# GpSimd masks the bias in seven of sixteen heads, conditions load packed, and the first values are projected behind the keys

## What is computed

```
emb = silu(sin_emb(timestep)) @ W_ada + b_ada         # timestep: one number a sample
scale, shift = split(emb)
h = ln(x) * (1 + scale) + shift
q, k, v = h @ Wq + bq, h @ Wk + bk, h @ Wv + bv       # 16 heads of 16
s = q k^T / sqrt(16) + attention_bias[b, head]        # 512 x 512 for each sample and head
s = where(mask[b], -inf, s)                           # one mask for all heads of a sample
x1 = h + softmax(s) v @ Wo + bo
```

## Time and profile before

| | us |
|---|---|
| three runs, median (lowest to highest) | 1149.35 (1147.81 to 1149.48) |
| the profiled execution | 1147.64 |
| its span, first to last instruction | 1145.8 |
| busy: PE, DVE, ACT, GpSimd | 1026.5, 818.1, 776.6, 349.4 |

### The profile page before, as it was taken

How to read it: one execution, slowest core, us unless ns; L and a number is a source line. 1 busy time by engine, 2 the same in 40 slices (tenths; PEclk the granted TensorE clock), 3 DMA queues, 4 the chain that set the end, 5 groups by cost and what they waited for, 6 DMA issues and landing times. The chain is left out here.

```text
span 1145.8 us, 21120 instructions
## 1 busy us (share of the span) xinstructions
PE 1026.5 (90%) x6128; PEld 670.0 (58%) x6128; DVE 818.1 (71%) x2056; ACT 776.6 (68%) x1238; POOL 349.4 (30%) x464
## 2 busy tenths in 40 slices
PE   2599999999999999999999999983999989898862
PEld 2456556656656565655655665642777767676641
DVE  5586775876787777778678686764456978897665
ACT  2287877887787788778788787863457565765442
POOL 0205114213312322320511511004455555654421
PEclk9799999999999999999999999996999999999976
DMA  7787976986995995896796797641111110101001
GB/s 237 241 299 262 353 274 232 367 294 225 338 326 191 340 349 204 305 356 233 275 362 245 250 371 266 247 151 37 38 37 38 37 55 18 55 18 37 19 19 37
DMA packets 131288, 230.23 MB, mean 201 GB/s; under 512 B 8992, under 2 KB 58016, under 8 KB 127136
## 3 DMA queue, kind: packets, MB, share of 16 engines
q1 hardware_dynamic: 131232, 229.59, 56.8%
HBM read 187.62 MB, written 41.94 MB: 200 GB/s over the span
## 5 line engine op out<-in xcount | busy, mean ns | idle before, releaser
L679 DVE CUSTOM_DVE_ANT_0 prob<-s_bank,big 128x512 f32<-128x512 f32 x512 | 344.8, 686 | 128.7 <-PE s_bank L540 103.0
L820 ACT ACTIVATE prob<-prob,nmax 128x512 f32<-128x512 f32 x512 | 359.6, 722 | 36.4 <-DVE nmax L679 35.2
L549 PEld LDWEIGHTS t_bank<-ident,prob 128*128 128x128 f32 x2048 | 241.0, 141 | 196.7 <-issue 71.2
L549 PE MATMUL t_bank<-ident,prob 128*128 128x128 f32 x2048 | 316.0, 277 | 8.0 <-DVE pt L688 4.7
L827 ACT COPY pt<-t_bank 128x512 f32<-128x512 f32 x320 | 185.1, 578 | 98.6 <-PE t_bank L549 98.0
L539 PE MATMUL s_bank<-stack_k,stack_q 128*128 128x512 bf16 x512 | 195.6, 382 | 4.6 <-DVE nmax L679 2.6
L540 PE MATMUL s_bank<-mterm_early,ident_bf 128*128 128x512 bf16 x448 | 170.8, 381 | 0.0
L688 DVE COPY pt<-t_bank 128x512 f32<-128x512 f32 x192 | 132.0, 687 | 48.9 <-PE t_bank L549 48.9
L562 PE MATMUL o_bank<-pt,val 128*32 128x512 f32 x1024 | 135.8, 604 | 0.7 <-ACT pt L827 0.7
L1624 POOL TENSOR_TENSOR gl<-big,gh 128x512 fp32r<-128x512 f32 x64 | 87.1, 1372 | 86.3 <-DVE gh L1329 86.3
L939 POOL TENSOR_SCALAR val<-vst 128x64 f32<-128x64 f32 x128 | 27.0, 245 | 251.8 <-PE o_bank L562 217.9
(11 more groups left out here) (176 smaller groups left out, 1620.1 us busy)
## 6 DMA issues: line engine op xcount, KB each, us to landing
big<-in_fside_Bx16xSxS SPq DMA_DIRECT2D x128, 1024.0 KB, 6.6
pieces_dram<-pieces SPq DMA_DIRECT2D x64, 384.0 KB, 7.8
stack_q<-pieces_dram SPq DMA_DIRECT2D x16, 1024.0 KB, 8.0
stack_k<-pieces_dram SPq DMA_DIRECT2D x16, 1024.0 KB, 8.7
pieces_dram<-pieces SPq DMA_DIRECT2D x32, 256.0 KB, 7.5
xin<-in_x SPq DMA_DIRECT2D x8, 512.0 KB, 6.6
x_dram<-x SPq DMA_DIRECT2D x8, 512.0 KB, 2.6
big<-x_dram SPq DMA_DIRECT2D x8, 512.0 KB, 3.5
```

Source lines behind the costliest of these rows:

```text
L549: last = pe.transpose(t_bank[n % 2][:, c * P:(c + 1) * P], prob[:, n % NT, c * P:(c + 1) * P], ident[:])
L679: dve.tensor_tensor_reduce(out=prob[:, n % NT, :], in0=s_bank[n % 3][:, :], in1=bias[:, h % NB, t, :], scale=-1.0, scalar=3e38, op0=ALU.ad ...
L820: act.activation(tile, tile, ACT.Exp, bias=nmax[:, n % NT:n % NT + 1], scale=-1.0).then_inc(exped.sem, 1)
```

## The change

Three things are changed; lines are those of the kernel before.

1. **Masking.** The heads 1, 2, 3, 12, 13, 14 and 15 get no mask product on TensorE. For them GpSimd adds the mask term to the head's bias in its buffer, one operation of 128x2048 (`mask_bias`), placed at iterations -3, 1, 6, 42, 46, 50 and 54 of GpSimd's order, and DVE waits for it in place of the bias's landing. There is one mask term left, made after step 56's value copies; it serves all of the sample.
2. **Conditions.** The host packs the token numbers into one array, and angles, frequencies, pairs and four bias vectors into another. Two DMAs in place of eight, and the three for bq, bk and bo go too. W_ada is loaded behind x and waited for by PE alone.
3. **First values.** Before the loop, DVE takes the values' banks between its cuts (V0 behind K0's, V1 behind Q1's), and the low part of Wv is made before them. PE's order is the same, but it no longer waits for DVE's last cut there.

```diff
+POOL_MASKED = [1, 2, 3, 12, 13, 14, 15]
+MASK_AT = [-3, 1, 6, 42, 46, 50, 54]
+PE_MASKED = [h for h in range(H) if h not in POOL_MASKED]
+TERM_AT = 56
...
     def load(sp):
-        for dst, src in conds:
-            sp.dma_start(dst, src).then_inc(cond_in, 16)
+        sp.dma_start(toks[:], d["toks"]).then_inc(vecs_in, 16)
+        sp.dma_start(vecs[:], d["vecs"]).then_inc(vecs_in, 16)
+
+    def load_weights(sp):
+        sp.dma_start(w_ada, v["W_ada"]).then_inc(w_ada_in, 16)
...
-        dve.wait_ge(cond_in, 16 * len(conds))
+        dve.wait_ge(vecs_in, 32)
...
             def load_mask(b):
-                sp.wait_ge(late_term.sem, late_term.at(b, QT))
+                sp.wait_ge(term_done.sem, term_done.at(b - 1, QT))
...
             def scores(b, n):
-                if n < QT:
-                    pe.wait_ge(early_term.sem, early_term.at(b - 1, n + 1))
-                if h == EARLY_HEADS:
-                    pe.wait_ge(late_term.sem, late_term.at(b, t + 1))
+                by_pe = h in PE_MASKED
+                if h == PE_MASKED[0]:
+                    pe.wait_ge(term_done.sem, term_done.at(b - 1, t + 1))
...
-                pe.matmul(bank, stack_q[:, h, t * P:(t + 1) * P], stack_k[:, h, :], start=True, stop=False)
-                pe.matmul(bank, ident_bf[:], mterm[:, t, :], start=False, stop=True).then_inc(scored.sem, 1)
+                last = pe.matmul(bank, stack_q[:, h, t * P:(t + 1) * P], stack_k[:, h, :], start=True, stop=not by_pe)
+                if by_pe:
+                    last = pe.matmul(bank, ident_bf[:], mterm[:, t, :], start=False, stop=True)
+                last.then_inc(scored.sem, 1)
...
             def add_bias(b, n):
-                if t == 0:
+                if t == 0 and h in POOL_MASKED:
+                    dve.wait_ge(masked.sem, masked.at(b, POOL_MASKED.index(h) + 1))
+                elif t == 0:
                     dve.wait_ge(bias_in[h % NB], b * (16 * H // NB) + 16 * (h // NB + 1))
...
-            for m, use in enumerate(banks.uses):
-                if use in VALUES:
-                    dve.wait_ge(weights_in, 16 * len(later))
...
+            spare_use(banks, at["XT", 0], -1, first=True)
+            spare_use(banks, at["XT", 1], -1, first=True)
+            low_parts(-1)
+            dve.wait_ge(weights_in, 16 * len(later))
+            dve.wait_ge(w_high, 3)
+            dve.tensor_tensor(wl["wv"][:], w["wv"], wh["wv"][:], ALU.subtract).then_inc(w_low, 1)
+            cut(0)
+            cut(1)
+            spare_use(banks, at["V", 0], -1, first=True)
+            cut(2)
+            spare_use(banks, at["V", 1], -1, first=True)
+            cut(3)
...
+            def mask_bias(b, h):
+                pool.wait_ge(bias_in[h % NB], b * (16 * H // NB) + 16 * (h // NB + 1))
+                if h == POOL_MASKED[0]:
+                    pool.wait_ge(term_done.sem, term_done.at(b - 1, QT))
+                apart(pool, pool_apart)
+                pool.tensor_tensor(bias[:, h % NB], bias[:, h % NB], mterm[:], ALU.add).then_inc(masked.sem, 1)
```

More of the change, by code:

```diff
@@ L90, in load_layouts @@
         v[w] = d["L0_cond_" + w].rearrange("(c p) n -> p c n", p=P)
-    for w in BY_FEATURE:
+    for w in BY_FEATURE[len(VECTORS):]:
         v[w] = d["L0_cond_" + w]
@@ L193, in sines_of @@
         act.wait_ge(sines, 1)
-        act.activation(k["trig"][:], arg[:], ACT.Sin).then_inc(sines, 1)
+        act.activation(k["trig"][:], arg, ACT.Sin).then_inc(sines, 1)
         act.wait_ge(sines, 2)
@@ L205, in modulate @@
         last.then_inc(ada_done, 1)
-    return dict(load=load, angles=angles, domains=domains, rotations=rotations, modulation=modulation,
+    return dict(load=load, load_weights=load_weights, angles=angles, domains=domains, rotations=rotations, modulation=modulation,
                 sines_of=sines_of, modulate=modulate)
@@ L942, in copy_values, with mask_term @@
                 last.then_inc(val_done.sem, 1)
-            def early_mask_term(b, t, first=False):
+            def mask_term(b, t, first=False):
                 if t == 0:
@@ L978, in iteration @@
                         copy_values(b, VALUES_AT.index(n))
-                    if n == LATE_TERM_AT:
+                    if n in MASK_AT:
+                        mask_bias(b, POOL_MASKED[MASK_AT.index(n)])
+                    if not last and n == TERM_AT:
                         for t in range(QT):
-                            late_mask_term(b, t, first=first)
-                    if not last and n == EARLY_TERM_AT:
-                        for t in range(QT):
-                            early_mask_term(b, t)
+                            mask_term(b, t)
+                    if not last and n - STEPS in MASK_AT:
+                        mask_bias(b + 1, POOL_MASKED[MASK_AT.index(n - STEPS)])
             for t in range(QT):
-                early_mask_term(-1, t, first=True)
+                mask_term(-1, t, first=True)
             pool.wait_ge(consts, 3)
@@ L991, in _ @@
             keep_residual(-1, first=True)
+            for h, n in zip(POOL_MASKED, MASK_AT):
+                if n < 0:
+                    mask_bias(0, h)
             iteration(0, first=True)
@@ L1751 @@
     place = np.arange(P) % 4
-    arrays["pairs"] = np.stack([place < 2, place >= 2], 1).astype(np.float32)
+    pairs = np.stack([place < 2, place >= 2], 1).astype(np.float32)
     beside = np.zeros((P, P), np.float32)
```

91 lines of the change are left out of this document (39 added, 52 removed).

## The result

| | before | after |
|---|---|---|
| median of four runs each (lowest to highest), us | 1148.58 (1147.48 to 1149.48) | 1121.86 (1121.42 to 1123.60) |
| the profiled execution; its span | 1147.64; 1145.8 | 1121.61; 1119.8 |
| busy: PE, DVE, ACT, GpSimd | 1026.5, 818.1, 776.6, 349.4 | 996.4, 816.5, 776.1, 558.8 |

The ratio is 0.977, interval 0.976 to 0.979: 26.7 us less between the medians and 26.0 between the profiled executions, where 31 were forecast. The page after, in order: span, busy time, the clock over forty slices, and the new group of GpSimd.

A forecast was written before the change was run, and what follows sets the result against it. TensorE was taken to bound attention, with ACT right behind it, already saturated in plain steps. Masking -20.5 and start -10.4 sum to -30.9 us: 1116.7 for the profiled execution, 1118.5 for the median, range 1101 to 1137.

The forecast's parts named there:

- Part 1: Attention: mask products leave TensorE in seven heads, gaining 2.7 us a sample (1.7 to 4.4), -20.5 us over 7.6 samples.
- Weighing steps: Iterations 1 to 4 and 49 to 52: PE alone sets them, so all eight products are paid, 1.73 us a sample.
- Iterations 5 to 12: Eight products beside spare transposes, output projection and ACT's table changes: gain 0.3 us a sample, bounds 0 and 1.3.
- Iterations 45 to 48 and 53 to 60: Twelve products in steps where ACT's 0.91 us outlasts PE's need: gain 0.7 us a sample, bounds 0 and 1.4.
- First sample: It has no weighing in steps 1 to 4, so it counts as 0.6 of a sample: -1.6 us.
- the clock falls: Rival: PE's clock drops in plain steps of heads 13 to 15, costing 4.2 us a sample, near 1150; chance 0.03.
- Part 2: GpSimd's seven additions a sample: 4.3 us each (4.1 to 5.2), within its deadlines, no charge for DVE contention.
- x up to 4.6: Heads 12 to 15: price in us of one GpSimd addition up to which four in a row meet step 60.
- Part 3 and 4: Start: packed conditions begin the chain 7.7 us earlier, values behind the keys gain 2.7; together -10.4 us (-5.5 to -11.4).
- TensorE bound to the end: Rival in attention: ACT has unseen slack, every mask product is paid, 48.4 us in all, 1090.5; chance 0.12.
- GpSimd takes the gain: Rival in attention: an addition costs 4.7 to 5.2 us, delays eat the 2.7 us, time 1139; chance 0.15.
- GpSimd becomes the bound: Rival: above 5.2 us an addition, a sample loses 7 x (x - 4.6), 1168 at x = 5.5; chance 0.07.

The follow-up runs named there:

- The four-head run: The changed kernel with GpSimd masking only heads 1, 13, 14 and 15, and heads 2, 3 and 12 back on TensorE: 1124.75 us, ratio 0.9801.
- the run with the new start alone: The changed kernel with masking as before the change; packed conditions and values behind the keys stay: 1138.57 us, ratio 0.991.
- the run without additions: The changed kernel with GpSimd's additions and the waits for them left out, so seven heads are not masked: 1119.27 us, ratio 0.9753.
- the ten-head run: The changed kernel with GpSimd masking heads 1, 4 to 9, 13, 14 and 15, without holding GpSimd back: 1141.97 us, ratio 0.9947.

## Why the prediction was right, point by point

The forecast was 1118.5, in 1101 to 1137; measured were 1121.9 and 1120.6.

**Part 1, the sum, was right; two of its terms were off in opposite directions.** The table has turns of PE after the first addition of the same sample (the one that begins at 319.4 before and at 305.07 after), as starts in PE's timeline.

| turn of step | before | after | gained in all |
|---|---|---|---|
| 4 | 10.31 | 9.50 | 0.81 |
| 13 | 22.07 | 20.63 | 1.44 |
| 48 | 73.86 | 72.41 | 1.45 |
| 52 | 81.92 | 79.60 | 2.32 |
| 57 | 86.75 | 83.57 | 3.18 |
| 58 | 87.73 | 85.32 | 2.41 |
| 61 | 90.92 | 88.19 | 2.73 |

- Weighing steps: 0.81 + 0.87 = 1.68, forecast 1.73. PE's price of a product, 0.216 and not 0.38, held.
- Iterations 5 to 12: 0.63, forecast 0.3. I had taken ACT as the limit there; part of the steps was PE's after all.
- Iterations 45 to 48 and 53 to 60: 0.0 and 0.4, forecast 0.7 together. In the first of them ACT has no gap, as forecast. In the second the forecast had ACT as the only bound; what it left out is DVE. At turn 57 the gain is 3.18, at turn 58 2.41: it is there for a moment and then taken back by the 0.83 us wait shown above, ahead of which ACT itself stood 0.64 us for DVE.

Sum 2.7, as forecast; that an error of 0.3 each way cancelled is luck. The four-head run agrees: 0.60 for heads 2, 3 and 12. ACT's rows without a gap, which I had named as a sign for heads 12 to 15, break at step 58.

**First sample, forecast -1.6, measured +1.1.** This is the step that failed. I priced it as 0.6 of a middle sample. That was right for the products: without the additions the sample takes 82.83, 1.9 less than before. Three things that I had not charged cost the other 3.0, each with its place in the table of additions. Two are deadlines, 0.7 at head 3 and 1.2 at head 12: I had worked them out in a middle sample alone, where DVE waits 0.2 and nothing, and in the first one it waits 0.76 and 1.14. A wait at head 12 was my own sign of being wrong, and here it is. The third, 1.1, is the lower clock in steps 18 to 20: the rival "the clock falls", at another place, and once in a launch rather than in every sample. In the run with the new start alone the same steps lose 1.7.

**Part 2, GpSimd's price.** I took 4.3 between 4.1 and 4.65; it measured 4.07 to 4.12. The lower end, 4.65 less three fixed parts of 0.18, was right, but not by its rows: a one-input operation of 1024 columns at 1.046 and one of 512 at 0.68 give a fixed part of 2 x 0.68 - 1.046 = 0.31 and a price of 3.7. That the 0.18 put in their place fits is luck. The room at head 12, 4.9, measured 5.15, and x up to 4.6 measured 4.8. The rule of the Trainium skill that DVE should do elementwise work ("GPSIMD Engine Reference", 3.1 Elementwise) speaks against this change; here GpSimd had three quarters of the sample idle, and its seven additions cost a middle sample nothing. What they would cost on DVE was not tried. Its 4497 ns for two fp32 operands is no measurement of this one, whose second operand is bf16. Head 1's wait was absorbed, as the run without additions shows (88.53 both). DVE's bias additions took 0.694 at most, as forecast; that operations with two SBUF inputs would be blocked, which I had set aside as not met here, was made visible by the ten-head run.

**Part 3 and 4, -7.7 and -2.7, -10.4 together.** Measured -10.2, and -10.6 in the run that has them alone. The conditions are there at 3.74 (I had 3.7 from DVE's own clearing), and the first score waits for stack_k, whose landing moved from 48.0 to 40.8, 7.2 earlier. The first addition came 4.3 behind that landing before and comes 1.3 behind it now: 3.0 for the new order of the values, where I had 2.7. PE now idles 8.80 before its first score, as I had said it would; the loss that I had counted there (0.6 of the 3.3) is not to be told in the first addition, and the first score and what follows to 43.7 run at the lower clock, as I had thought they might; before the change the clock was down from 51.6 to 55.0, at the first scores too.

**The rivals.** *TensorE bound to the end* (1090.5) fell: PE waits for ACT, and ACT for DVE, in plain steps, and even without any mask a sample takes 83.7. *GpSimd takes the gain* fell with the price of 4.1. *GpSimd becomes the bound* was right as a mechanism: with 5.3 the formula gives 1149 + 8 x (7 x 0.7 - 4.0) = 1156, measured 1154.9. Its formula leaves out the clock, which is a part of that time; so that it comes so near is partly luck.

**The network stage**, forecast unchanged, ran 1.9 longer in the profiled execution. Among the profiled executions of all the kernels here it took 381.8 to 385.7 us from the last addition to the end, though its code is the same in all, and the two of the changed kernel took 383.7 and 382.6. The clock stood at 0.50 for 69.2 us of it in the first of these, for 65.8 in the second and for 63.4 before the change. So 1.1 of the 1.9 is scatter between single executions of one kernel; the rest is not explained. Together with the first sample it is the distance to the forecast: 2.7 + 1.9 = 4.6 of 30.9 - 26.0 = 4.9.

## What to carry to other kernels

Price an instruction on the bounding engine start to start, and only in the steps where that engine has no one behind it: here 28 products of 0.216 gave 2.7 us and not 6.05, since ACT needs 0.91 us in a plain step in which PE had needed 0.87, and DVE, which I had not counted, holds ACT up behind the weighing steps. Count every engine behind the bound, with its odd jobs and its order. Work that goes to an idle engine is free up to a deadline, and the first and the last iteration have deadlines of their own. Before giving GpSimd more long operations, list the DVE operations with two SBUF inputs beside them; one wait that kept them apart was worth 34 us.

## What was new about the hardware

- A GpSimd addition of 128x2048, fp32 and bf16 to fp32, takes 4.07 to 4.12 us, where one of 512 columns takes 1.16. By an estimate from the two, (4 x 1.161 - 4.102) / 3, about 0.18 of each is fixed.
- DVE's subtraction of 128x512 with two SBUF inputs takes 2.33 to 4.55 us beside such additions, and 0.68 to 0.70 when kept apart. Two in a row took 6.8 us together, since GpSimd began its next addition before the second of them could start.
- Behind a stretch in which PE did little the granted clock fell to the 1.2 GHz level for 3.4 us (first sample, at 60.8) or 6.9 us (ten heads, at 349.9). The second is dearer than the stall seems: 4.78 us of waiting, and then transposes at 1.12 instead of 0.66. With PE busy for 1.15 of 3.40 us (67.8 to 71.2) the kernel before kept its clock, so a stretch of low work does not settle it.
